# Sixteen shared tiles ahead of a scatter: rows copied in SBUF, and the scatter held back until six tiles are done

## The reference, cut to what matters

```
scores = sigmoid(x @ gate_w)                       # 2048 tokens, 32 experts
...
g = ragged_dot(xs, w_gate, group_sizes)            # xs: rows sorted by expert
u = ragged_dot(xs, w_up, group_sizes)
d = ragged_dot(silu(g) * u, w_down, group_sizes)
expert_out = sum(d[unsort_idx].reshape(T, K, H) * weights[..., None], axis=1)
shared = silu(x @ sw_gate) * (x @ sw_up) @ sw_down
return expert_out + shared
```

## Time and profile before

| what | value |
|---|---|
| median of 3 runs | 2575.61 us |
| the profiled execution's own time | 2570.16 us |
| its span (first to last instruction) | 2568.4 us |
| PE busy | 2042.9 us, 80% |
| POOL busy | 1078.8 us, 42% |
| mean granted TensorE clock | 0.885 of full |

### The profile page before, as it was taken

How to read it: one execution, slowest core, us unless ns; L and a number is a source line. 1 busy time by engine, 2 the same in 40 slices (tenths; PEclk the granted TensorE clock), 3 DMA queues, 4 the chain that set the end, 5 groups by cost and what they waited for, 6 DMA issues and landing times. The chain is left out here.

```text
span 2568.4 us, 34881 instructions
## 1 busy us (share of the span) xinstructions
PE 2042.9 (80%) x10592; PEld 1472.8 (57%) x10593; DVE 1125.2 (44%) x2087; ACT 536.7 (21%) x1139; POOL 1078.8 (42%) x558
## 2 busy tenths in 40 slices
PE   6925887968827799986232999999999999999873
PEld 3403443433313333335121899999999999899763
DVE  2573451076645567743610333333333333333466
ACT  2300221101113444420010121212112112121110
POOL 0000000005543556630175057676577787820355
PEclk8967997989966899996565999999999999999886
DMA  3061005021232333410364235555445555622466
GB/s 103 0 172 56 17 25 204 1 76 66 82 136 84 116 126 139 146 47 3 119 260 172 70 101 169 165 156 174 149 144 174 177 177 169 187 75 82 141 198 180
DMA packets 196665, 310.57 MB, mean 121 GB/s; under 512 B 16976, under 2 KB 95584, under 8 KB 196352
## 3 DMA queue, kind: packets, MB, share of 16 engines
q1 hardware_dynamic: 127296, 175.57, 21.2%
q10 hardware_dynamic: 53952, 83.91, 10.2%
q0 software_dynamic: 15360, 50.34, 5.9%
HBM read 196.51 MB, written 113.25 MB: 121 GB/s over the span
## 5 line engine op out<-in xcount | busy, mean ns | idle before, releaser
L2053 PE MATMUL psum<-e_gu_high,e_rowT_high 128*128 x1280 | 438.7, 344 | 23.5 <-issue 14.9
L2053 PE MATMUL psum<-e_gu_low,e_rowT_high 128*128 x1280 | 417.6, 329 | 0.8 <-issue 0.8
L2053 PEld LDWEIGHTS psum<-e_gu_high,e_rowT_high 128*128 128x128 f32 x1280 | 246.9, 193 | 56.3 <-issue 52.1
L1861 ACT ACTIVATE e_silu<-psum 128x352 f32<-128x352 f32 x160 | 74.2, 463 | 976.8 <-PE psum L2058 834.1
L2058 PE MATMUL psum<-e_gu_high,e_rowT_low 128*128 x1280 | 262.1, 327 | 6.8 <-issue 6.7
L2053 PEld LDWEIGHTS psum<-e_gu_low,e_rowT_high 128*128 128x128 f32 x1280 | 247.6, 193 | 7.2 <-issue 3.6
L2073 PE MATMUL psum<-e_d_high,e_midT_high 128*128 (+3 forms) x480 | 193.4, 403 | 53.3 <-issue 45.0
L1941 DVE TENSOR_TENSOR e_midT_low<-psum,e_midT_high 128x256 fp32r<-128x256 f32 x160 | 67.9, 424 | 376.9 <-ACT e_midT_high L1870 324.7
L2058 PEld LDWEIGHTS psum<-e_gu_high,e_rowT_low 128*128 128x128 f32 x1280 | 218.9, 192 | 7.0 <-issue 7.0
L1802 POOL TENSOR_TENSOR e_gu_high<-e_gu_in,e_ones 128x1408 fp32r<-128x1408 f32 x32 | 81.1, 2535 | 290.0 <-PE psum L2058 290.0
L2073 PE MATMUL psum<-e_d_low,e_midT_high 128*128 (+3 forms) x480 | 191.8, 400 | 0.0
(11 more groups left out here) (329 smaller groups left out, 3790.8 us busy)
## 6 DMA issues: line engine op xcount, KB each, us to landing
d_sorted<-y_zeros SPq DMA_DIRECT2D x32, 1024.0 KB, 6.9
e_row<-d_sorted ACTq DMA_DIRECT2D x128, 256.0 KB
d_y<-e_y ACTq DMA_DIRECT2D x128, 256.0 KB, 3.2
e_gu_in<-in_L_ffn_w_gate SPq DMA_DIRECT2D x32, 704.0 KB
e_gu_in<-in_L_ffn_w_up SPq DMA_DIRECT2D x32, 704.0 KB
e_d_in<-in_L_ffn_w_down SPq DMA_DIRECT2D x32, 512.0 KB
e_row<-d_hs ACTq DMA_DIRECT2D x32, 256.0 KB
e_d_in<-in_L_ffn_w_down SPq DMA_DIRECT2D x32, 192.0 KB
```

The source lines that it names most:

```text
L2053: nc.tensor.matmul(bank[:, 0:M].unsqueeze(1), rowT_high[par][:, k, :], w[:, bass.ds(buffer, 1), k, at:at + M], start=(k == 0 and part == 0 ...
```

## The change

Four things change in `expert_tiles`; nothing else in the program does.

- ACT's `load` from `d_hs` for tiles 0 to 15 becomes `copy_row`, an ACT copy from `hs` in SBUF into the same buffer. It runs two tiles ahead, after the turned row has been copied.
- ACT's first loop runs over tiles 2 to 13 in place of 2 to 11.
- POOL waits for `y_copied` to reach 6 before its first scatter.
- SP issues the loads of experts 0 and 1 in straight-line code, then waits for `scattered`, loads sorted rows 0 and 1 itself, and only then enters its loop from expert 2. ACT's own wait for `scattered` goes.

```diff
@@ def _(sp):
+            def expert(e):
                 load(e + 1, *(c.dram[w][bass.ds(e, 1)].rearrange("a k n -> (a k) n")
                               for w in ("L1_ffn_w_gate", "L1_ffn_w_up", "L1_ffn_w_down")))
+
+            shared(0, 0, again=False)
+            for e in range(2):
+                expert(e)
+            sp.wait_ge(scattered, NT * TOPK * 16)
+            for par in range(2):
+                sp.wait_ge(row_turned, NT - 1 + par)
+                sp.dma_start(row[par][:].unsqueeze(1), sorted_tiles[:, par:par + 1, :]).then_inc(row_loaded[par], 16)
+            with sp.Fori(2, E_) as e:
+                expert(e)
             shared(E_ + 1, 1)
@@ def _(pool):
             pool.wait_ge(ones_set, 1)
+
+            pool.wait_ge(y_copied, 6)
             for t in range(NT):
                 for k in range(TOPK):
                     nc.gpsimd.indirect_dma_start(c.dram["d_sorted"], ...
@@ def _(act):
+            def copy_row(t, par):
+                nc.scalar.copy(row[par][:].unsqueeze(1), hs[:, bass.ds(t, 1), :]).then_inc(row_loaded[par], 16)
...
+                if ahead is not None:
+                    copy_row(ahead, par)
...
-            load(hs_tiles, 0, 0)
-            load(hs_tiles, 1, 1)
+            copy_row(0, 0)
+            copy_row(1, 1)
             copy_rowT(0, 0)
-            load(hs_tiles, 2, 0)
             high_parts(0)
             for i in range(2):
-                steps(i, i, source=hs_tiles, t=i + 3, stores=False, old=(i > 0))
+                steps(i, i, stores=False, old=(i > 0), ahead=i + 2)
             high_parts(1)
-            with act.Fori(1, NT // 2 - 2) as n:
+            with act.Fori(1, NT // 2 - 1) as n:
                 for par in range(2):
-                    steps(n * 2 + par, par, source=hs_tiles, t=n * 2 + par + 3, stores=False)
-            for i in range(NT - 4, NT + 2):
-                if i + 3 < NT:
-                    steps(i, i % 2, source=hs_tiles, t=i + 3, stores=False)
+                    steps(n * 2 + par, par, stores=False, ahead=n * 2 + par + 2)
+            for i in range(NT - 2, NT + 2):
+                if i + 1 < NT:
+                    steps(i, i % 2, stores=False)
                 else:
-                    if i + 3 == NT:
-                        act.wait_ge(scattered, NT * TOPK * 16)
                     steps(i, i % 2, source=sorted_tiles, t=i + 3 - NT, stores=False)
```

More of the change, by code:

```diff
@@ L1755, in expert_tiles @@
             nc, c, "e_", "midT_high_ready midT_low_ready down_done y_copied")
+        hs_tiles = c.dram["d_hs"].rearrange("(t p) d -> p t d", p=P)
+        sorted_tiles = c.dram["d_sorted"].rearrange("(t p) d -> p t d", p=P)
+        y_tiles = c.dram["d_y"].rearrange("(t p) d -> p t d", p=P)
         block = stack.enter_context(nc.Block())
@@ L1776, in shared @@
                 load(n, c.dram["L1_ffn_sw_gate"][:, part], c.dram["L1_ffn_sw_up"][:, part], c.dram["L1_ffn_sw_down"][part, :], again)
-            shared(0, 0, again=False)
-            with sp.Fori(0, E_) as e:
+            def expert(e):
                 load(e + 1, *(c.dram[w][bass.ds(e, 1)].rearrange("a k n -> (a k) n")
                               for w in ("L1_ffn_w_gate", "L1_ffn_w_up", "L1_ffn_w_down")))
+            shared(0, 0, again=False)
[7 more added lines that the diff above has]
+                expert(e)
             shared(E_ + 1, 1)
@@ L1848, in pieces @@
                                                    (d_in[0:LAST_M, 2, :], d_high[0:LAST_M, par, 2, :], d_low[0:LAST_M, par, 2, :])]))
-        hs_tiles = c.dram["d_hs"].rearrange("(t p) d -> p t d", p=P)
-        sorted_tiles = c.dram["d_sorted"].rearrange("(t p) d -> p t d", p=P)
-        y_tiles = c.dram["d_y"].rearrange("(t p) d -> p t d", p=P)
         @block.scalar
@@ L1874, in store, with steps @@
                 act.dma_start(y_tiles[:, bass.ds(i - NT, 1), :], y[par][:].unsqueeze(1)).then_inc(y_stored[par], 16)
-            def steps(i, par, more=True, source=None, t=None, stores=True, old=True):
+            def steps(i, par, more=True, source=None, t=None, stores=True, old=True, ahead=None):
                 silus(i, par)
```

## The result

The changed kernel took 2578.93 us (median of 14 runs), the kernel before 2572.05 (14 runs beside them): ratio 1.0021, interval [1.0013, 1.003], so 5.4 us slower (3.3 to 7.7). I had forecast 10 us slower. Later batches of runs (a batch is a group of runs made on one chip, one after another) brought a second result that I had not foreseen at all: in four of seven batches the kernel before takes only some 2471 us, and in the one of these in which the changed kernel ran too (batch 4) it is 1.8% slower, not 0.2%. Two executions lie far outside everything else and count in no ratio: one of the kernel before in batch 4 (7043.8 us) and one of e15 (3135.3 us). First the profile of the changed kernel from the first batch.

A forecast was written before the change was run, and what follows sets the result against it. PE was taken as the bound, its completions draining at one matmul in 2.75 us under the scatter. Silu of tile 16 at 1513.5 against 1503.3 made 10 us later: 2580 profiled, 2586 us against the median, range 2546 to 2596.

The forecast's parts named there:

- The deciding row: Silus of tiles 8 to 10: 50 us and more apart confirms the forecast, 6.69 us hiding, 15 to 25 mild drain.
- Start of the stage: Before the scatter: weights land 5 us earlier, 5 us of set 1's split on the path; first scatter at 1335.
- The progress under the scatter: Tiles while PE drains: from tile 7.6 at 1341 to tile 10 at 1469, 2.0 tiles plus 0.4.
- The tile behind the scatter: After the release at 1469: one tile at half clock, 11 us, bringing tile 11.
- The onset: Start of PE's draining under the scatter: within 6 us of a burst's start, so full speed to about 1341.
- code run for the first time: Reason behind the hiding rival: engines stalled at tile 2 in first-run code, loops cure it; hiding's chance 0.18.
- the scatter hides: Rival: 16 tiles finish before the scatter ends, silu of tile 16 at 1475, 28 us earlier, 2548 us; chance 0.18.
- The mild drain: Rival: scatter drains PE as gently as the gather, 0.47 us a transpose, 25 us earlier, 2550 us; chance 0.20.

The follow-up runs named there:

- e15: Changed kernel with six indirect DMAs behind each tile instead of one burst, beside a kernel before of 2569.73 us: 2515.74 us, ratio 0.9795.
- e1: Kernel before without the 96 indirect DMAs of the scatter and the waits for them: 2462.52 us, ratio 0.9576.
- e4: Changed kernel without POOL's wait, the 96 scatters replaced by plain DMAs issued by SP behind expert 0's weights: 2469.8 us, ratio 0.9594.
- e5: Changed kernel without POOL's wait, the 96 scatters replaced by plain DMAs of the same size issued by POOL: 2478.82 us, ratio 0.9629.
- e3: Changed kernel without POOL's wait, plus 28 extra 704 KB loads by SP beside the scatter: 2472.15 us, ratio 1.0014.
- e18: Same edit as e3 (no POOL wait, 28 extra loads beside the scatter), run again in another batch: 2472.98 us, ratio 1.0006.
- e10: The changed kernel again without any edit, beside a kernel before of 2470.04 us: 2514.86 us, ratio 1.0181.
- e9: Changed kernel with 96 indexed reads into an unused SBUF tile in place of the scatter, sort left out: 2514.8 us, ratio 1.0176.
- e8: Changed kernel with scatter rows of 256 bytes (64 of 512 columns), as many indirect DMAs: 2509.92 us, ratio 1.0167.
- the paced kernel: Changed kernel with all 96 indirect DMAs, six at a time, POOL waiting for one more tile before each later group; first measured as e7, 2465.29 us.
- e7: Changed kernel with six indirect DMAs at a time, the first two groups at once, each later one behind one more tile: 2465.29 us, ratio 0.9975.
- e11: Same edit as e7 on the changed kernel, run again beside a kernel before of 2470.04 us: 2464.39 us, ratio 0.998.
- e12: Same edit as e8 on the changed kernel (scatter rows of 256 bytes), run again: 2512.3 us, ratio 1.018.

## Why the forecast was right in its mechanism and wrong in its size

Shown, in the late condition in which the forecast was made and measured: with the scatter PE's completions reach ACT and DVE late, and without it (e1) or with plain DMAs in its place (e4, e5) they don't; the scatter does so in loops as in straight code; starting it six tiles later moves the hole and does not shrink it. The deciding row that I had named, silus of tiles 8 to 10 more than 50 us apart with "remote" before them, is there for tile 9 (1347.30, 1444.07), with the clock at 0.56; tile 10 came 27 us behind it, when the scatter had ended.

What failed is the sum: I put the silu of tile 16 10.2 us later, and it came 6.0 us later (5.4 by the medians). Three terms were mis-sized, the start of the stage, the progress under the scatter and the tile behind it. All marks from the stage's start:

| mark | forecast | measured |
|---|---|---|
| silu of tile 1 | 18.7 | 16.5 |
| silu of tile 6 | 56.7 | 51.8 |
| first scatter | 61.7 | 58.3 |
| last scatter (its start) | 182.7 | 179.0 |
| silu of tile 10 | 195.7 | 193.6 |
| silu of tile 11 | 206.7 | 202.5 |
| silu of tile 16 | 240.2 | 235.95 |

**Start of the stage.** I took 5 us for the weights landing earlier (bounds 0 to 10); silu of tile 1 came 2.1 us earlier still (7.1 us earlier than before, counted from the stage's start). I put 5 us of set 1's split on the path; tiles 1 to 6 took 35.3 us, against 33.5 for five at 6.69, so it is 1.8. The two put silu of tile 6 4.9 us earlier than forecast; POOL's release came 6.5 us behind it, not 5, so 3.4 us earlier, and the last issue 3.7. **The progress under the scatter** gave 1.6 us of this back: silu of tile 10 came 14.6 us behind the last issue, where I had 13. **The tile behind the scatter** took 8.85 us (1471.04 to 1479.89), not 11: I had carried over 11.85 from the kernel before, where DVE's split of set 1 stood in it. The onset, which I had put 6 us after the first issue, came between 5 and 7 us after it. Together: 3.7 less 1.6 and 2.15 more make the 4.2 us that silu of tile 16 came earlier than forecast, and 10.2 less 4.2 is the 6.0 measured. That they add up to no more is in part luck: the progress under the scatter was carried over from a single stall, with 0.4 of a tile added by feel, and its error had the opposite sign to the other two.

The forecast also rested on a condition that I did not know of. The range of 2546 to 2596 us holds only late batches; the 2514.9 us of the changed kernel in batch 4 lie outside it. The result stayed inside it because the runs behind the forecast and those of the result had the same condition, and not by anything in the argument.

**The rivals.** That code run for the first time stalls the engines is refuted by e1, and by late handovers inside loops. The Trainium skill, "Runtime: NRT & Kernel Launch", section "Instruction fetch mechanics", thus explains nothing here. "SBUF — State Buffer", section "Who interferes with whom", has that PE and ACT never wait on anyone. It speaks of SBUF ports. In the prompt batch nothing waits (PE busy 45 of 45 us); in the late one PE is busy 14 of 105 us, because ACT and DVE get its completions late, and whether a port has a part in that no run here shows. The rival "the scatter hides" I had worked out to a silu of tile 16 at 1475, bound by the scatter's end; in batch 4 it came at 1471.64. But the 28 us faster that I gave it holds only for the reason that I had named, code run for the first time, which would stall the kernel before and not the changed one. If nothing holds PE back, nothing does in the kernel before either, and then the later start costs most of its 54 us (last scatter at 179.0 against 124.6 us from the stage's start): 45 us slower was measured. The traces of e3 and e18, prompt and with the scatter at once, agree: silu of tile 16 at 149.6 and 151.4 us from the stage's start, against 193.9 in e10. The mild drain at 2550 us did not occur with an unbroken scatter; that the gather is mild because of its pauses is suggested by e15 and not shown, since e9, its unbroken counterpart, ran in a prompt batch only.

**Open.** What makes a batch late or prompt: chip 7 had each once, and inside a batch the runs of the kernel before agree within 17 us, while the conditions lie 100 apart. Which part of the indexed DMA does it (index reading, row addresses, bytes): e8 and e9 never met a late batch. Whether plain traffic beside it helps, and with it whether plain DMAs by POOL would be harmless beside half idle DMA engines too. By what path an indirect DMA holds back a completion of PE. What the 0.2 to 0.4% of the paced kernel in prompt batches come from. There is no trace of the kernel before from a prompt batch, so its 2471 us are not taken apart.

## What to carry to other kernels

Where indirect DMAs run beside TensorE work as here, don't issue them in one unbroken burst, and don't start them late either: start at once and let the issuing engine wait for each tile (e7). Against the kernel before that is 2.0% faster in the late batch (2515.7 against 2569.7 us) and 0.2 to 0.4% in three prompt ones, while the changed kernel is slower than it in both conditions. Before comparing times across batches, look which condition each had; here it makes 4%. And a rival of the form "this mechanism isn't there" has to be applied to both kernels, before and after, ahead of giving its time.

## What the runs showed of the hardware

The kernel before took 2470.0 us in one batch and 2569.7 in another on the same chip (7). Two traces of the changed kernel, one of either condition (after, e10), have the scatter issued at the same pace and at 204 to 207 GB/s; the difference is when PE's finished matmuls are seen by ACT and DVE. The paced kernel on chip 7 took 2464.4 us prompt (e11) and 2515.7 late (e15). Ninety-six plain DMAs by POOL with the same packets and bytes (7680, 25.17 MB), issued in 50.6 us beside full DMA engines, made no completion of PE late in a batch in which the indexed ones cost 110 us. POOL needs 0.54 us to issue a plain DMA of 128 rows, and 0.96 us with 0.30 between two for an indexed one; rows of 256 bytes instead of 2 KB are issued no faster (e12: 96 in 120.2 us).
